# Feed-forward weights folded during the last recurrent steps, and the first item's products around the last output chain

## The reference

```python
def step(carry, inp):                       # 8 chunks of 64 tokens, per head
    w0_, w1_, w2_ = carry
    ...                                     # gradients, newtonschulz5 on each
    w0_ = w0_ / (jnp.linalg.norm(w0_, axis=1, keepdims=True) + 1e-05) * w0n
    ...
    oi = silu(qi @ w0_) * (qi @ w2_) @ w1_
    return ((w0_, w1_, w2_), oi)
...
out = out * jax.lax.rsqrt(jnp.mean(out * out, axis=-1, keepdims=True) + 1e-05) * onorm_w
return out @ W_proj

# feed-forward, SCALE = 64, fwht = Walsh-Hadamard transform / sqrt(n)
x = fwht(x * SU_ug) / SCALE
x_up = x @ W_up.T * (Wscale_ug[:INTER] * SCALE)
x_gate = x @ W_gate.T * (Wscale_ug[INTER:] * SCALE)
x = jax.nn.silu(x_gate) * x_up
x = fwht(x * SU_dp) / SCALE
x = x @ W_down.T * (Wscale_dp * SCALE)
```

## Time and profile before

| | us |
|---|---|
| median of 3 runs | 1163.43 (1163.25 to 1165.26) |
| the profiled execution, its own time | 1163.57 |
| its span, first to last instruction | 1161.8 |
| TensorE busy | 1062.6 (91%) |
| VectorE busy | 711.6 (61%) |
| ScalarE busy | 557.6 (48%) |
| GpSimd busy | 425.5 (37%) |
| mean granted TensorE clock | 0.948 |

### The profile page before, as it was taken

One profiled execution on the slowest core, in us unless ns is written; L12 is line 12 of the kernel. 1 busy time (PEld: TensorE's weight loads), 2 busy tenths in 40 slices (PEclk: granted clock), 3 DMA queues, 4 the chain that ended last, 5 costly groups with the idle time before them and its releaser, 6 DMA issues.

```text
span 1161.8 us, 25494 instructions
## 1 busy us (share of the span) xinstructions
PE 1062.6 (91%) x10006; PEld 764.4 (66%) x10006; DVE 711.6 (61%) x2080; ACT 557.6 (48%) x1427; POOL 425.5 (37%) x374
## 2 busy tenths in 40 slices
PE   5989999999989739999999899999999999999667
PEld 2647888888888624656556758676767676667335
DVE  4329889988997653122222666756675757575853
ACT  2447787788776514121213354545354545444321
POOL 1022212331321153001012555656575647574530
PEclk8689999999998769999999999999999999999879
DMA  9200000000000042200002100300030003002002
GB/s 341 103 1 1 3 0 0 0 0 0 1 2 1 2 102 95 118 1 0 1 1 62 30 19 21 73 19 19 21 73 20 19 22 72 20 19 93 1 1 73
DMA packets 24204, 42.15 MB, mean 36 GB/s; under 512 B 6576, under 2 KB 14768, under 8 KB 22704
## 3 DMA queue, kind: packets, MB, share of 16 engines
q1 hardware_dynamic: 24112, 40.87, 11.9%
HBM read 21.98 MB, written 2.10 MB: 21 GB/s over the span
## 4 chain that ended last, share of the span: by engine, by line
PE 54%; DVE 7%; ACT 2%; issue 1%; POOL 0%; DVEq 0%; ACTq 0%
PE quad L1657 9%; PE quad L1728 9%; PE bank L1770 7%; PE quad L1790 6%; PE bank L1773 5%; PE quad L1801 5%; PE bank L1670 5%; DVE norm_xn L1337 2%; PE quad L1736 1%; ACT act_probs L2020 1%; ACT act_probs L2027 1%; PE quad L1844 1%; PE bank L1689 1%; PE bank L1844 1%; DVE act_probs L2131 1%
## 5 line engine op out<-in xcount | busy, mean ns | idle before, releaser
L2378 POOL TENSOR_TENSOR act_probs<-act_probs,rden 128x512 f32<-128x512 f32 (+3 forms) x128 | 171.1, 1340 | 173.7 <-DVE rden L2150 173.6
L2020 ACT ACTIVATE act_probs<-act_probs,neg_max 128x256 f32<-128x256 f32 (+3 forms) x256 | 140.8, 552 | 86.8 <-DVE neg_max L2131 86.6
L1728 PEld LDWEIGHTS quad<-hT,ug_raw_switch 128*128 128x128 f32 x1024 | 120.0, 193 | 30.2 <-issue 18.3
L1728 PE MATMUL quad<-hT,ug_raw_switch 128*128 128x128 f32 x1024 | 131.7, 283 | 3.0 <-ACT act_probs L2027 2.2
L2131 DVE CUSTOM_DVE_ANT_0 act_probs<-bank,mask 128x256 f32<-128x256 f32 (+3 forms) x256 | 115.2, 486 | 7.2 <-PE bank L1773 6.9
L1657 PE MATMUL quad<-hT,ug_queries 128*128 128x512 f32 x256 | 113.6, 595 | 0.0
L1770 PE MATMUL bank<-ckvT,ug_queries 64*128 64x512 f32 (+3 forms) x512 | 105.0, 479 | 6.6 <-DVE neg_max L2131 6.6
L2150 DVE RECIPROCAL rden<-den 128x2 f32<-128x2 f32 x128 | 20.6, 161 | 119.8 <-ACT act_probs L2020 119.6
L2111 DVE SCALAR_TENSOR_TENSOR act_probs<-quad,ws_up,silu_keys 128x512 f32<-128x512 f32 x32 | 24.0, 751 | 102.7 <-ACT silu_keys L1985 102.7
L1657 PEld LDWEIGHTS quad<-hT,ug_queries 128*128 128x128 f32 x256 | 47.6, 190 | 55.3 <-issue 55.1
L1985 ACT ACTIVATE silu_keys<-quad,ws_gate 128x512 f32<-128x512 f32 x32 | 22.0, 687 | 125.4 <-PE quad L1657 125.4
(11 more groups left out here) (369 smaller groups left out, 2477.8 us busy)
## 6 DMA issues: line engine op xcount, KB each, us to landing
rope_swapped<-gate SPq DMA_DIRECT2D x120, 64.0 KB, 2.0
wmod<-in_wmod SPq DMA_DIRECT2D x2, 1536.0 KB, 9.9
x_pairs<-in_x SPq DMA_DIRECT2D x2, 1024.0 KB, 9.9
x_rows<-x_pairs SPq DMA_DIRECT2D x8, 256.0 KB, 5.0
wq_wo<-in_wq_nopeT SPq DMA_DIRECT2D x1, 2048.0 KB, 7.3
wq_wo<-in_wo SPq DMA_DIRECT2D x1, 2048.0 KB, 11.2
down_keys<-x_pairs SPq DMA_DIRECT2D x16, 128.0 KB, 2.3
ug_raw_switch<-in_switch_w SPq DMA_DIRECT2D x1, 2048.0 KB, 7.5
```

The costliest lines, as they stand in the source:

```text
L1728: mm = nc.tensor.matmul(out[:, P * i:P * i + P], w[:, kt, HP * half + i, :], k.hT[:, kt, b, cols], start=(kt == 0), stop=(kt == KT - 1))
L2020: nc.scalar.activation(tile, tile, ACT.Exp, bias=neg_max[:, r, e:e + 1], scale=-1.0, accum_out=den[:, r, e:e + 1])\
L2378: nc.gpsimd.tensor_tensor(tile, tile, rden[:, t % RING, :].unsqueeze(2).to_broadcast([P, 2, cols]), ALU.mult)\
```

## The change

The fold of the weights moves into steps 5 to 7 and `finish`. It is done in place: `fly_up` and `fly_down`, both on GpSimd, replace `butterfly` and `fold_down`, and the folded weights stay in `ug_raw_switch` and `down_raw_out`. `fly_up(0)` stands behind GpSimd's work of step 5, `fly_up(1)` behind that of step 6, `fly_down` (10 instructions) and the product of gates and scales behind that of step 7, ahead of `add_out(6)`. Folds 0 to 2 are made at the end of step 6, folds 3 and 4 in step 7, the others in `finish`. The first item's norm takes the places that q, k of the next chunk leave empty in step 7.

The new `finish` weaves the output chain of the last chunk with `up(0, 0)` to `up(0, 7)` and their gates and products. The chain uses banks 4 to 7 instead of bank 6 alone. The square root on ScalarE becomes a mean on VectorE and a power on GpSimd. `stage_rest` begins with `down_product(0)`, with the second item's norm between its halves; the first four `absorb` stand two by two ahead of `up(1, 6)` and `up(1, 7)`; SP issues `wq_loads` right behind the moves to `x_rows`. Buffers change names: what was in `ug_queries` is in `ug_raw_switch` and the other way round, the same for `down_keys` and `down_raw_out`, and gradients, squares and `a_bf` lie in `act_probs` and `silu_keys`.

```diff
@@ TensorE, end of step(t)
-                turn_weight(t, 3)
-                turn_weight(t, 4)
-                if ahead:
-                    project_qk(1, [1])
-                turn_weight(t, 0)
-                turn_weight(t, 1)
+                elif more:
+                    pe.wait_ge(s["qkv_taken"], 3 * (t + 2))
+                    for f in range(3):
+                        if f < 2:
+                            begin(QK_BANK[f], WN)
+                        ffn.fold(pe, f, bank[FOLD_BANK[f]])
...
+            def finish(t):
+                pe.wait_ge(ffn.had_taken, 5)
+                ffn.fold(pe, 5, bank[7])
+                for f, q in ((6, 5), (7, 2)):
+                    pe.wait_ge(taken[q], PH * t + WN)
+                    ffn.fold(pe, f, bank[q])
+                for q in (0, 1):
+                    pe.wait_ge(taken[q], PH * t + WN)
+                ffn.up(pe, 0, 0)
+                turn_weight(t, 3, TURN_BANK[3])
+                pe.wait_ge(ffn.had_taken, 7)
+                turn_weight(t, 4, TURN_BANK[4])
+                pe.wait_ge(s["proj_taken"], NCH)
+                turn_weight(t, 0, TURN_BANK[0])
+                turn_weight(t, 1, TURN_BANK[1])
+                pe.wait_ge(ffn.had_taken, 8)
+                pe.wait_ge(taken[3], PH * t + WN)
+                ffn.up(pe, 0, 1)
+                pe.wait_ge(taken[3], DONE)
+                turn_weight(t, 5, TURN_BANK[5])
+                pe.wait_ge(taken[4], DONE)
+                turn_weight(t, 2, TURN_BANK[2])
+                pe.wait_ge(s["q_moved"], NCH)
+                pe.wait_ge(taken[0], DONE)
+                for j in range(2):
+                    out_product(0, j)
+                ffn.up(pe, 0, 2)
+                pe.wait_ge(taken[1], DONE)
+                for j in range(2):
+                    out_product(1, j, at=7)
+                ffn.up(pe, 0, 3)
+                for q in (5, 2):
+                    pe.wait_ge(taken[q], DONE)
+                out_rows(t, 4)
+                ffn.up(pe, 0, 4)
+                pe.wait_ge(s["out_silued"], NCH)
+                ffn.fold(pe, 8, bank[6])
+                pe.wait_ge(s["out_hidden"], NCH)
+                ffn.fold(pe, 9, bank[7])
+                turn_out(t, 5)
+                ffn.up(pe, 0, 5)
+                project_out(t, 4)
+                for f in (10, 11):
+                    pe.wait_ge(ffn.had_taken, f - 1)
+                    ffn.fold(pe, f, bank[FOLD_BANK[f]])
+                ffn.up(pe, 0, 6)
+                ffn.up(pe, 0, 7)
@@ ScalarE
+            def finish(t):
+                ffn.take_fold(act, 7, bank[FOLD_BANK[7]])
+                ffn.gate(act, 0, 0)
+                for q in (3, 4, 0, 1):
+                    take_weight(t, q, TURN_BANK[q])
+                ffn.gate(act, 0, 1)
+                for q in (5, 2):
+                    take_weight(t, q, TURN_BANK[q])
+                silu_out(t)
+                ffn.gate(act, 0, 2)
+                ffn.gate(act, 0, 3)
+                square_out(t, 4)
+                ffn.gate(act, 0, 4)
+                for f in (8, 9):
+                    ffn.take_fold(act, f, bank[FOLD_BANK[f]])
+                take_out(t, 5)
+                ffn.gate(act, 0, 5)
+                take_proj(t, 4)
+                for f in (10, 11):
+                    ffn.take_fold(act, f, bank[FOLD_BANK[f]])
+                ffn.gate(act, 0, 6)
+                ffn.gate(act, 0, 7)
@@ VectorE
+            def finish(t):
+                ffn.product(dve, 0, 0)
+                ffn.product(dve, 0, 1)
+                ffn.product(dve, 0, 2)
+                hidden_out(t, 7)
+                ffn.product(dve, 0, 3)
+                mean_out(t)
+                ffn.product(dve, 0, 4)
+                norm_out(t, 4)
+                for m in range(5, MT):
+                    ffn.product(dve, 0, m)
@@ GpSimd
+            step(NCH - 3)
+            pool.wait_ge(k.ffn_in, N_FFN)
+            pool.wait_ge(s["h_copied"], NCH)
+            ffn.fly_up(pool, 0)
             step(NCH - 2, ahead=False)
+            ffn.fly_up(pool, 1)
             step(NCH - 1, more=False, ahead=False)
+            pool.wait_ge(s["qkv_summed"], 3 * NCH)
+            ffn.fly_down(pool, down_spare)
+            nc.gpsimd.tensor_tensor(k.gates[0][:], k.gates[0][:], k.ws_dp[:].unsqueeze(1).to_broadcast([P, B, D]), ALU.mult)\
+                .then_inc(ffn.down_flown, 1)
             add_out(NCH - 2)
+            invert_out(NCH - 1)
             add_out(NCH - 1)
...
+    def fly_down(self, pool, spare):
+        add = self.k.nc.gpsimd.tensor_tensor
+        low, high = self.w_down[:, 0:self.SPLIT], self.w_down[:, self.SPLIT:MT]
+        add(spare, low, high, ALU.add).then_inc(self.down_flown, 1)
+        pool.wait_ge(self.down_flown, 1)
+        add(high, low, high, ALU.subtract).then_inc(self.down_flown, 1)
+        n = 2
+        for src, to, step in ((spare, low, 2), (high, spare, 2), (low, high, 1), (spare, low, 1)):
+            pool.wait_ge(self.down_flown, n)
+            ...
+            add(plus, a, b, ALU.add).then_inc(self.down_flown, 1)
+            add(minus, a, b, ALU.subtract).then_inc(self.down_flown, 1)
+            n += 2
@@ stage_rest, TensorE
+            down_product(0, [0, 1])
             for kt in range(KT):
+                norms.turn(pe, LN0B + 1, kt, bank[6 + kt])
+            down_product(0, [2, 3])
```

More of the change, by code:

```diff
@@ L804, in step @@
                         project_v(t + 2, [n])
+                    elif ph == PROJECT_V and not more and n in (0, 2):
+                        if n == 0:
+                            pe.wait_ge(norms.taken, norms.done(LN0B, 1))
+                        else:
+                            pe.wait_ge(ffn.had_taken, 4)
+                        ffn.fold(pe, 3 + n // 2, bank[7])
                     elif ph == TURN_OUT and not first:
@@ new lines, in step @@
+                if more:
+                    turn_weight(t, 3)
+                    turn_weight(t, 4)
+                    if ahead:
+                        project_qk(1, [1])
+                    turn_weight(t, 0)
+                    turn_weight(t, 1)
+            def finish(t):
[45 more added lines that the diff above has]
+                ffn.up(pe, 0, 7)
@@ L837, in pe_program @@
             step(NCH - 1, more=False, ahead=False)
[L838 to L853 removed]
+            finish(NCH - 1)
         def act_program(act):
@@ L986, in step @@
                 root_state(1)
+                if not more:
+                    for f in (5, 6):
+                        ffn.take_fold(act, f, bank[FOLD_BANK[f]])
                 root_state(0)
@@ L1180, in dve_program @@
             step(NCH - 1, more=False)
-            hidden_out(NCH - 1)
-            norm_out(NCH - 1)
+            finish(NCH - 1)
         def pool_program(pool):
```

393 lines of the change are left out of this document (200 added, 193 removed).

## The result

The changed kernel takes **1130.99 us** in the median of 4 runs (1128.36 to 1132.08), the kernel before 1163.34 us beside it: a ratio of 0.9717, 95% interval 0.9695 to 0.9739. The forecast was 1123.8 us with a range of 1117 to 1131: the median lies at the very edge of the range, and 32.4 us were gained instead of 39.6. The profiled execution took 1128.36 us with a span of 1126.6 us, 4.5 us above what was forecast for it (1123.9 us). The other 2.6 us of the median are the difference of the other three runs from that one; two of them show a mean granted clock of 0.959 instead of 0.963.

A forecast was written before the change was run, and what follows sets the result against it. The first 52 us behind the recurrence were bounded by chains where TensorE waits, the rest by TensorE. Moving `down_product(0)` from 475.88 to 435.3 us, less 0.9, saves 39.7 us: 1123.9, median 1123.8 us; range 1117 to 1131.

The forecast's parts named there:

- rival 3: Seam of steps 6 and 7: folds don't hold the clock, the 3.1 us aren't gained; 1126.9 us, chance 0.10.
- rival 4: Step 7: folds stand in the recurrence's way, five ScalarE takes exposed, seam gain lost; 1130.3 us, chance 0.06.
- The seam: Steps 6 and 7: folds 0 to 2 fill TensorE's hole and gain 3.1 us; bounds 0 and 3.1.
- Inside step 7: First norm's work and folds 3 and 4 in step 7 lose 0.8 us; bounds 0 and 2.
- `fly_down`: End of step 7: GpSimd's instructions block three VectorE squares, final weights 4.2 us later; bounds 0 and 4.7.
- rival 1: End of step 7: squares not blocked by `fly_down`, transposes done 3.8 us earlier; 1120.0 us, chance 0.20.
- `finish`: Transposes end at 397.3 us, TensorE's list runs 35.9 us at full clock, `down_product(0)` starts at 435.3 us.
- rivals 2 and 5: Clock falls ahead of `finish`, 1128.3 us, chance 0.17; clock stays low in it, 1163.6 us and above, chance 0.02.
- its hole ahead of `turn_out`: In `finish`, `norm_out` behind `product(0,4)` makes `turn_out` wait 2.3 us; folds cover 1.7, leaving 0.7 us.
- The rest unchanged: Behind `down_product(0)`: only 0.9 us of added transposes, otherwise nothing changes; 686.8 us to the end.
- the moved transposes: The next norm's 8 transposes, formerly ahead of `down_product(0)`, now stand inside it and cost 0.9 us.

The follow-up runs named there:

- after, again: The changed kernel itself, unaltered, run and profiled once more: 1130.09 us, ratio 0.9709.
- fly_down later: The changed kernel with GpSimd's `fly_down` moved behind `add_out(6)` and the gates' product behind `add_out(7)`: 1124.38 us, ratio 0.9665.
- fly_down later, again: The kernel of "fly_down later" repeated on another chip, beside "both edits, again": 1124.59 us, ratio 0.9666.
- no clash: On top of "fly_down later", `add_out(6)` also waits for the last `scale_state`: 1126.42 us, ratio 0.9672.
- third norm later: The changed kernel with the transposes and `modulate` of the third item's norm one `up` later: 1128.16 us, ratio 0.9685.
- seam filled: The kernel before with three matmuls of 512 columns, results unread, in the hole of the seam of steps 6 and 7: 1160.08 us, ratio 0.9962.
- chain filled, wide: The kernel before with unneeded matmuls of 0.87 us in TensorE's holes from the seam through output chain and setup: 1165.12 us, ratio 1.0012.
- chain filled, half: As "chain filled, wide" on the kernel before, with fillers half as wide, 0.43 us each: 1157.50 us, ratio 0.9942.
- in sequence: The changed kernel with six `up` products behind the output chain in `finish` instead of woven into it: 1134.26 us, ratio 0.9734.
- both edits: The changed kernel with the edits of "fly_down later" and "third norm later" together: 1125.24 us, ratio 0.9660.
- both edits, again: The kernel of "both edits" repeated on the next chip, beside "fly_down later, again": 1121.00 us, ratio 0.9627.

## Why the prediction was right, and where it was off

The forecast's number was nearer to a miss than its mechanism: of the 7.2 us between 1123.8 and 1130.99 us none lies in the edited stretch. That the median is still in the range is luck. The upper end of the range, 1131 us, was set for rivals 3 and 4, and neither took place; what filled the room were low clocks elsewhere, for which the prediction had no term.

The stretches of all the profiles together (microseconds; "low" is the time behind `down_product(3)` that TensorE spent at the lower clock, summed from windows of 2 us):

| kernel | first turn | to down_product(0) | to down_product(3) | to the end | low |
|---|---|---|---|---|---|
| before | 350.16 | 125.72 | 154.46 | 531.46 | 31 |
| after | 352.21 | 84.65 | 157.12 | 532.62 | 31 |
| after, again | 351.98 | 84.64 | 157.11 | 532.47 | 34 |
| fly_down later | 350.30 | 82.44 | 157.04 | 531.52 | 27 |
| fly_down later, again | 351.40 | 82.42 | 156.84 | 531.34 | 31 |
| no clash | 351.85 | 82.41 | 156.89 | 535.65 | 38 |
| third norm later | 351.56 | 84.63 | 153.58 | 536.63 | 41 |
| seam filled | 352.68 | 117.00 | 154.46 | 531.16 | 31 |
| chain filled, wide | 351.69 | 125.43 | 154.46 | 531.42 | 31 |
| chain filled, half | 350.00 | 114.87 | 154.47 | 536.66 | 41 |
| in sequence | 352.38 | 89.78 | 158.81 | 536.53 | 41 |
| both edits | 351.52 | 82.42 | 153.58 | 531.28 | 27 |
| both edits, again | 352.82 | 82.43 | 153.59 | 532.66 | 34 |

*The seam*: 3.1 us forecast, 3.2 found, and the run with the seam filled shows that they are the clock's. GpSimd's `fly_up` costs nothing, as forecast: from the first turn of the seam before to this one it is 39.03 us in the kernel before (350.16 - 311.13) and 39.03 us in the changed one (352.21 - 313.18).

*Inside step 7*: 0.8 us forecast, bounds 0 and 2. The first square comes 33.50 us behind the first turn (385.71 - 352.21), in the kernel before 35.47. The seam alone takes 3.16 off that, so 1.2 us are lost. On TensorE `project_out` comes 34.77 us behind the first turn (386.98 - 352.21) instead of 35.95, a loss of 2.0 us. The term was undersized by 0.4 us for VectorE and 1.2 for TensorE.

*`fly_down`*: it ran from 372.05 to 387.29 us and the gates to 389.66; the end of both was forecast at 388.0 us, or 390.05 with the 2.05 us by which this execution lies later. The squares were blocked, so rival 1 fell, and by 3.4 us instead of 4.2. The step behind it was right in its result and off in one link: `up(0,0)` was expected to be held up by the updates queued behind the squares. These ended at 391.2 us, 0.1 us before the folds did, so it ran right behind the folds, as it does with the squares free (391.34 - 352.21 = 39.13 us behind the first turn, and 389.44 - 350.30 = 39.14 in the experiment). The first transposes, ready at about the same time, stand behind it from 394.90 us on. So there were two paths of nearly equal length, and the price of the block on the way to the end was 2.2 us. The 3.8 us of the first rival were the distance between turns done at 393.5 and at 397.3 us. Counted from 350.16 us as the first turn, they are done at 394.5 us with the squares free, since TensorE's side was undersized in step 7, and at 396.7 us with them blocked, since the block was oversized.

*`finish`*: turns done at 397.3 us forecast, 398.74 - 2.05 = 396.7 found; the list 35.9 us forecast, 434.87 - 398.74 = 36.1 found; its hole ahead of `turn_out` 0.7 and 0.45 us; the last gate, product and the end of the block 2.1 forecast, 2.0 found. The clock was 1.00 throughout, so rivals 2 and 5 fell; rival 3 fell with the seam, and of rival 4 no more is left than the 1.2 us by which TensorE lost more in step 7. That the sum is within 0.5 us is in part errors that cancel: the block 0.8 us too large, the losses of step 7 too small. The 41.1 us that the stretch lost can be divided by the runs, in this one order: 10.9 for the clock alone (chain filled, half), 25.1 for the folds and the norm in the holes of step 7 and of the chain, with what clock and smaller changes of the chain go with them (114.87 to 89.78), and 5.1 for the interleaving of `up`. In another order the shares could differ.

*The rest unchanged*: here the forecast failed, by 2.9 us in the profiled run. It had named the sign: 686.8 us from `down_product(0)` to the end, where 689.7 were found. It put 0.9 us for the moved transposes, which were found, and nothing else. The third item's hole, the same 2.5 us in every kernel that has it, is followed by a low clock in all six profiles of the changed kernel and of those built on it (156.8 to 157.1 us between the down products, and 158.8 with `finish` in sequence, which has the low clock at `down_product(0)` too) and in none of the four of the kernel before and of those built on it (154.46 or 154.47 us). That is 1.8 us, and by these ten profiles it comes with the edit. Why the clock stays up behind the one and not behind the other, with the same products around both, is not settled: moving the norm removes hole and loss together and says nothing of the cause.

*The bottom and the top*: from `down_product(3)` to the end the profiles take 531.2 to 536.7 us, in two groups that follow the low clock (27 to 34 us of it: 531.2 to 532.7; 38 to 41 us: 535.7 to 536.7) and not the edit: before and after have 31 both, and both groups have kernels of either family. The first turn lies between 350.0 and 352.8 us in the same way. The kernel before happened to be profiled with the short values of both, 350.16 and 531.46, and the forecast took these as the kernel's. The three profiles of kernels built on it (350.0 to 352.7 and 531.2 to 536.7 us) show that some microseconds of the total move between executions. The runs spread accordingly: those of the kernel before over 2.5 to 6.8 us, depending on the chip, those of the changed kernel over 3.7 and 6.6. This is where the 2.6 us between the profiled run and the median belong, as far as is known.

## What to carry to other kernels

In this kernel a stage in which TensorE waits cost twice, once for the wait and once for the lower clock of the thin work around it. Filling its holes with useful work from the next stage got both. A filler that computes nothing measures the second share by itself, as long as it is narrower than its hole: at 0.43 us each it did, at 0.87 us the fillers became the path. A sum over a written instruction list at full clock was right within 0.5 us in 85, in part by errors that cancel; what was missed lay outside it, in stretches "unchanged" by the edit whose clock was not. So profile the kernel before twice, and give the range a term for the clock of the rest. And when a wait is removed, the gain is the distance to the next path: here 2.2 us of 3.4, and 0 of 2.2 for the second clash.

## What the runs showed of the hardware

- A square of 128x128 with an accumulator, 0.28 us by itself, took up to 2.43 us beside a GpSimd instruction of 2.42 us and ended 0.14 us behind it. GpSimd's additions gave way less: 1.55 and 1.60 us beside `scale_state` instead of 1.27, while the last four `scale_state` went from 0.68 to 1.2 us in the mean.
- The same 2.5 us of waiting, behind the same products, left the clock at 1.00 in four profiles of one family and was followed by 0.50 in all six of the other that had it.
- TensorE's lower clock in the stage behind `down_product(3)` covered 27 to 41 us, depending on the execution, for the same instructions. With 38 to 41 us of it the stretch took 535.7 to 536.7 us, with 27 to 34 us 531.2 to 532.7.
